# Layer 2 feed-forward of a four-layer transformer kernel, rewritten as one pipeline over sixteen units

## The reference

```python
x = x + _L2_ffn_ref(_layernorm(x, axis=-1), L2_ffn_w1, L2_ffn_conv_w, L2_ffn_conv_b, L2_ffn_w2)

def act_quant(x):                       # per token: 8 bit levels
    scale = 127.0 / jnp.clip(jnp.max(jnp.abs(x), axis=-1, keepdims=True), 1e-05)
    return jnp.clip(jnp.round(x * scale), -128, 127) / scale
def weight_quant(w):                    # -1, 0, 1 times one level
    scale = 1.0 / jnp.clip(jnp.mean(jnp.abs(w)), 1e-05)
    return jnp.clip(jnp.round(w * scale), -1, 1) / scale
# bit_linear(x, w) = act_quant(x) @ weight_quant(w).T
h = bit_linear(x, w1)                   # 128 features -> 512
h = depthwise_conv1d(h.transpose(0, 2, 1), conv_w, conv_b)   # 3 taps along the tokens of a sequence
h = jax.nn.silu(h.transpose(0, 2, 1))
return bit_linear(h, w2)                # 512 -> 128
```

## Time and profile before

| | us |
|---|---|
| median of 3 runs | 3416.47 |
| the profiled execution | 3413.9 |
| its span on the core | 3412.1 |
| from the first turn of the layer norm (2868.53) to the end of the last addition to xT (3047.40) | 178.9 |
| one chunk of 448 tokens (2968.00 to 3008.20) | 40.2 |
| VectorE busy in that chunk | 25.2 |
| TensorE busy in that chunk, at a granted clock of 0.50 | 15.3 |

### The profile page before, as it was taken

The page is one execution under the profiler, slowest core; times in us unless marked ns, Lnnn a source line. Parts: engine busy times, 40 slices in busy tenths (PEclk is TensorE's granted clock), DMA queues, the critical chain, the costliest instruction groups (busy, mean ns, idle before and its releaser), DMA issues. The chain is left out here.

```text
span 3412.1 us, 74955 instructions
## 1 busy us (share of the span) xinstructions
PE 3079.0 (90%) x30282; PEld 2137.9 (63%) x30282; DVE 2292.5 (67%) x4268; ACT 1742.8 (51%) x2862; POOL 1869.8 (55%) x1048
## 2 busy tenths in 40 slices
PE   7979989999999999999979998899999995349969
PEld 5654556777777777777757777455555553236644
DVE  4555557777777777777644443799999985654455
ACT  4534325666656666665644454366666663114545
POOL 0004556777777777777642220588888872014427
PEclk9979988999999999999989999799999996559989
DMA  7730016776666667767514665433333321304600
GB/s 142 145 114 22 1 37 125 139 147 130 134 137 142 130 134 139 142 131 140 111 51 154 235 236 218 98 99 98 96 96 92 92 69 36 55 0 93 135 1 12
DMA packets 607380, 367.70 MB, mean 108 GB/s; under 512 B 462933, under 2 KB 566626, under 8 KB 606786
## 3 DMA queue, kind: packets, MB, share of 16 engines
q1 hardware_dynamic: 607042, 362.96, 46.1%
HBM read 174.41 MB, written 75.24 MB: 73 GB/s over the span
## 5 line engine op out<-in xcount | busy, mean ns | idle before, releaser
L1742 POOL TENSOR_TENSOR L_plo<-L_p,L_phi 128x1500 bf16<-128x1500 f32 x224 | 659.1, 2943 | 295.0 <-DVE L_phi L1819 295.0
L1699 ACT COPY L_ptlo<-L_lt 128x1536 bf16<-128x1536 bf16 x224 | 322.1, 1438 | 407.6 <-PE L_lt L1623 407.6
L2121 ACT ACTIVATE L2b_p<-L2b_score 125x448 f32<-125x448 f32 x768 | 378.7, 541 | 273.2 <-PE L2b_score L2034 272.0
L1637 PE MATMUL L_acc<-L_chi,L_pthi 125*128 125x128 bf16 x2688 | 462.1, 219 | 0.0
L1639 PE MATMUL L_acc<-L_chi,L_ptlo 125*128 125x128 bf16 x2688 | 461.4, 219 | 0.0
L1638 PE MATMUL L_acc<-L_clo,L_pthi 125*128 125x128 bf16 x2688 | 461.2, 219 | 0.0
L1808 DVE TENSOR_SCALAR_CACHE_REDUCE L_p<-L_score,L_cols 128x1500 f32<-128x1500 f32 x224 | 395.4, 1765 | 84.8 <-PE L_score L1615 84.6
L1819 DVE CAST L_phi<-L_p 128x1500 bf16<-128x1500 f32 x224 | 298.1, 1331 | 164.6 <-ACT L_p L1693 163.7
L1693 ACT ACTIVATE L_p<-L_p,L_least 128x1500 f32<-128x1500 f32 x224 | 346.5, 1547 | 67.0 <-DVE L_p L1808 63.1
L2164 POOL TENSOR_TENSOR L2b_psum<-L2b_p 125x896 f32<-125x896 f32 x128 | 266.8, 2084 | 131.0 <-ACT L2b_p L2121 128.6
L2191 DVE TENSOR_REDUCE L2b_max<-L2b_m 112x1 f32<-112x1000 f32 x256 | 300.7, 1195 | 17.2 <-PE L2b_m L2015 9.5
(11 more groups left out here) (635 smaller groups left out, 6890.8 us busy)
## 6 DMA issues: line engine op xcount, KB each, us to landing
L2b_kst<-L_keys SPq DMA_DIRECT2D x96, 375.0 KB, 5.6
L_ct<-L_ct SPq DMA_DIRECT2D x32, 768.0 KB
L2a_ct<-L_ct SPq DMA_DIRECT2D x32, 768.0 KB, 15.1
L_ctx<-dram_ctx SPq DMA_DIRECT2D x32, 750.0 KB
L_keys<-L2a_kout SPq DMA_DIRECT2D x32, 750.0 KB, 8.0
L_values<-L2a_vout SPq DMA_DIRECT2D x32, 750.0 KB
L2b_vin<-L_values SPq DMA_DIRECT2D x32, 750.0 KB
L0x_ctx<-dram_ctx SPq DMA_DIRECT2D x32, 672.0 KB
```

What stands on the lines that cost most here:

```text
L1637: pe.matmul(acc, w_hi[0:KP, t, :], v_hi[0:KP, t, :], start=(t == 0), stop=False)
L1699: act.copy(pt_lo[g % 2][:, :, :], lt_ps[:, 0:KT * 128].rearrange("p (t q) -> p t q", t=KT)).then_inc(lo_read, 1)
L1742: pool.tensor_tensor(p_lo[g % 2][:, :, 0:KP], probs[g % RP][:, :].rearrange("q (t k) -> q t k", t=KT), p_hi[g % 2][:, :, 0:KP], ALU.subtra ...
L2121: act.activation(probs[t % RP][:, half * 2 * GW:(half + 1) * 2 * GW], score_ps[half][0:KP, 0:2 * GW], ACT.Exp).then_inc(exp_done, 1)
```

## The change

The three blocks become one, and the hardware loop is written out.

- **Front.** The layer norm's rows are not turned back as such. They are quantised where they lie (one token per partition, `quantise_rows`), in two halves of 8 and 6 tiles, and the rounded levels, in bf16, are turned (L2797 of the new file). The inverse scales of all tokens are spread at once: GpSimd makes 14 diagonals, TensorE multiplies them with ones, ScalarE reads four results into `inv_wide`. Weight quantisation and the clearing of the padded tiles lie among these steps; GpSimd also makes twelve 128x128 diagonals of the taps.
- **Taps.** The three taps of a unit (one block `j` of one chunk; 16 units) are three f32 products on TensorE with those diagonals, accumulated in PSUM. ScalarE applies Silu with the bias as it reads them.
- **Second quantisation.** Nothing is turned but one 128x448 tile per chunk: ScalarE writes the magnitudes of the four hidden blocks, VectorE takes their elementwise maximum, TensorE turns it, VectorE reduces it and makes two diagonals, TensorE spreads scale and inverse scale over the partitions, and VectorE scales and rounds the hidden values as they lie. The second product then leaves features on the partitions, and goes to `xT` without a turn.
- **Order.** One loop over m = 0 to 23 on every engine: units 0 to 15 in front, and behind them the quantisation of the chunk before and the product of the one before that.

```diff
--- before.py
+++ after.py
@@
-                    pe.wait_ge(silu_done, 4 * ch + 4)
-
-                    def to_tokens(k):
-                        wait(pe, quant2, 4 * ch + k - 1)
-                        for j in range(4):
-                            m = pe.transpose(zt_ps[k % 2][0:TOK, j * 128:(j + 1) * 128],
-                                             conv[j][:, k * TOK:(k + 1) * TOK], c["ident"][:, :])
-                        m.then_inc(zt_done, 1)
...
+                def up(m):
+                    ch, j = divmod(m, HID)
+                    pe.wait_ge(q1_ready, tiles_of(ch))
+                    wait(pe, pad_ready, m - 1)
+                    pe.matmul(up_ps[m % 2][:, 0:CH], wq[0][:, j * 128:(j + 1) * 128], q1T[:, cols(ch)], start=True,
+                              stop=True).then_inc(up_done, 1)
+
+                def conv(m):
+                    j = m % HID
+                    pe.wait_ge(pad_ready, m + 1)
+                    wait(pe, silu_done, m - 1)
+                    for t in range(3):
+                        ins = pe.matmul(conv_ps[m % 2][:, 0:CH].rearrange("p (b s) -> p b s", b=NB), taps[:, j, t, :],
+                                        pad[m % 4][:, :, t:t + S], start=(t == 0), stop=(t == 2))
+                    ins.then_inc(conv_done, 1)
...
+                def wide2(ch):
+                    pe.wait_ge(diag2_ready, ch + 1)
+                    wait(pe, scaled_done, HID * ch)
+                    wait(pe, inv2_read, ch)
+                    for ps, diag in ((scale_ps, diag_s), (inv_ps, diag_i)):
+                        ins = pe.matmul(ps[:, 0:CH], c["ones"][0:TOK, :], diag[:, :, :].rearrange("p k t -> p (k t)"),
+                                        start=True, stop=True)
+                    ins.then_inc(wide2_done, 1)
+
+                def product(ch):
+                    wait(pe, y_scaled, ch)
+                    for j in range(HID):
+                        pe.wait_ge(q2_ready, HID * ch + j + 1)
+                        ins = pe.matmul(y_ps[:, 0:CH], wq[1][:, j * 128:(j + 1) * 128], q2[j][:, :], start=(j == 0),
+                                        stop=(j == HID - 1))
+                    ins.then_inc(y_done, 1)
...
+                pe.wait_ge(wide1_read, NCH)
+                pe.wait_ge(w_ready, 2)
+                pe.wait_ge(taps_ready, HID)
+                pe.wait_ge(last_rows, 1)
+                up(0)
+                for m in range(UNITS + 2 * HID):
+                    ch, j = divmod(m, HID)
+                    if front(m + 1):
+                        up(m + 1)
+                    if front(m):
+                        conv(m)
+                    if j == 2 and 1 <= ch <= NCH:
+                        turn_largest(ch - 1)
+                    if j == 2 and ch >= 2:
+                        product(ch - 2)
+                    if j == 3 and 1 <= ch <= NCH:
+                        wide2(ch - 1)
...
+                def silu(m):
+                    ch, j = divmod(m, HID)
+                    act.wait_ge(conv_done, m + 1)
+                    wait(act, scaled_done, HID * (ch - 2) + j + 1)
+                    act.activation(hid[ch % 2][j][:, :], conv_ps[m % 2][:, 0:CH], ACT.Silu, bias=cb[:, j:j + 1]
+                                   ).then_inc(silu_done, 1)
+
+                def magnitude(m):
+                    ch, j = divmod(m, HID)
+                    act.wait_ge(silu_done, m + 1)
+                    wait(act, largest_step, 3 * (ch - 1) + max(j, 1) if ch else 0)
+                    act.activation(size[j][:, :], hid[ch % 2][j][:, :], ACT.Abs).then_inc(size_done, 1)
...
+                def quantise_rows(h):
+                    a, b = halves[h]
+                    st.link(dve.tensor_reduce(top1[:, a:b], rows[:, a:b, :], AX.X, ALU.max, apply_absolute_value=True))
+                    st.link(dve.tensor_scalar(top1[:, a:b], top1[:, a:b], 1e-5, None, ALU.max))
+                    dve.tensor_scalar(inv1[:, a:b], top1[:, a:b], 1.0 / 127.0, level[:, 0:1], ALU.mult, ALU.mult
+                                      ).then_inc(inv1_ready, 1)
+                    st.link(dve.reciprocal(scale1[:, a:b], top1[:, a:b]))
+                    st.link(dve.tensor_scalar(scale1[:, a:b], scale1[:, a:b], 127.0, None, ALU.mult))
+                    st.link(dve.tensor_tensor(rows[:, a:b, :], rows[:, a:b, :],
+                                              scale1[:, a:b].rearrange("p (t o) -> p t o", o=1
+                                                                       ).broadcast_to([128, b - a, D]), ALU.mult))
+                    dve.tensor_scalar(rounded[:, a:b, :], rows[:, a:b, :], MAGIC, MAGIC, ALU.add, ALU.subtract
+                                      ).then_inc(rounded_ready, 1)
...
+                def scales(ch):
+                    dve.wait_ge(largest_turned, ch + 1)
+                    st.link(dve.tensor_reduce(top2[:, :], largest_ps[0:TOK, :].rearrange("p (k d) -> p k d", k=NT), AX.X,
+                                              ALU.max, apply_absolute_value=True))
+                    st.link(dve.tensor_scalar(top2[:, :], top2[:, :], 1e-5, None, ALU.max))
+                    dve.tensor_scalar(inv2[:, :], top2[:, :], 1.0 / 127.0, level[0:TOK, 1:2], ALU.mult, ALU.mult)
+                    st.link(dve.reciprocal(scale2[:, :], top2[:, :]))
+                    st.link(dve.tensor_scalar(scale2[:, :], scale2[:, :], 127.0, None, ALU.mult))
+                    for diag, values in ((diag_s, scale2), (diag_i, inv2)):
+                        ins = dve.tensor_tensor(
+                            diag[:, :, :],
+                            c["ident"][0:TOK, 0:TOK].rearrange("p (o t) -> p o t", o=1).broadcast_to([TOK, NT, TOK]),
+                            values[:, :].rearrange("p (k o) -> p k o", o=1).broadcast_to([TOK, NT, TOK]), ALU.mult)
+                    ins.then_inc(diag2_ready, 1)
...
+                def scale_hidden(ch):
+                    dve.wait_ge(wide2_done, ch + 1)
+                    for j in range(HID):
+                        dve.tensor_tensor(scaled[j][:, :], hid[ch % 2][j][:, :], scale_ps[:, 0:CH], ALU.mult
+                                          ).then_inc(scaled_done, 1)
+
+                def round_hidden(ch):
+                    for j in range(HID):
+                        dve.wait_ge(scaled_done, HID * ch + j + 1)
+                        dve.tensor_scalar(scaled[j][:, :], scaled[j][:, :], MAGIC, MAGIC + 127.0, ALU.add, ALU.min
+                                          ).then_inc(grown_done, 1)
...
+                padded(0)
+                for m in range(UNITS + 2 * HID):
+                    ch, j = divmod(m, HID)
+                    if front(m + 1):
+                        padded(m + 1)
+                    if m >= 2 and front(m - 2):
+                        enlarge(m - 2)
+                    if j == 3 and 1 <= ch <= NCH:
+                        scales(ch - 1)
+                    if j == 3 and ch >= 2:
+                        output(ch - 2)
+                    if j == 0 and ch >= 2:
+                        scale_hidden(ch - 2)
+                    if j == 1 and ch >= 2:
+                        round_hidden(ch - 2)
```

More of the change, by code:

```diff
@@ L2748, in chunks @@
-        def chunks(eng, chunk):
-            chunk(0)
-            with eng.Fori(1, NCH) as ch:
-                chunk(ch)
+        made, pads_zero, taps_ready = sem("made"), sem("pads_zero"), sem("taps_ready")
+        w_summed, w_total_ready, level_ready, w_ready = sem("w_summed"), sem("w_total"), sem("level"), sem("w_ready")
+        turned, stats_done, parts_done, var_ready, rstd_ready, offset_ready = [
+            sem(n) for n in ("turned", "stats_done", "parts_done", "var_ready", "rstd_ready", "offset_ready")]
@@ L2910, in _, with statistics @@
-                for j in range(4):
-                    dve.memset(pad[j][:, :, :], 0.0)
-                dve.tensor_copy(ident_b[:, :], c["ident"][:, :]).then_inc(made, 1)
-                dve.wait_ge(made, 1)
-                chunks(dve, chunk)
+                st = Steps(dve, step)
+                def statistics(h):
+                    for g in (2 * h, 2 * h + 1):
+                        t0, n = groups[g]
+                        dve.wait_ge(turned, g + 1)
+                        for t in range(n):
+                            ins = dve.bn_stats(stats[:, t0 + t, :], x_ps[g][:, t * 128:(t + 1) * 128])
+                    ins.then_inc(stats_done, 1)
@@ new lines, in _ @@
+                ins.then_inc(w_summed, 1)
+                statistics(0)
+                variance(0)
+                statistics(1)
+                dve.wait_ge(w_total_ready, 1)
+                dve.tensor_scalar(level[:, :], inv_ps[:, 0:2], 1.0 / COUNT, 1e-5, ALU.mult, ALU.max
+                                  ).then_inc(level_ready, 1)
+                a, b = halves[0]
+                dve.wait_ge(rstd_ready, 1)
+                dve.scalar_tensor_tensor(offset[:, a:b], total[:, a:b], -0.5, rstd[:, a:b], ALU.mult, ALU.mult
```

(16 more changed lines are left out.)

381 lines of the change are left out of this document (195 added, 186 removed).

## The result

The changed kernel takes 3330.4 us (median of 4 runs, 3329.1 to 3331.5) against 3416.3 for the kernel before (4 runs, 3412.0 to 3417.1): a ratio of 0.9751, 95% interval 0.9739 to 0.9764. The profiled execution takes 3331.2, its span is 3329.2 and its mean clock 0.95. The forecast was 3335.6.

The account below looks back on a forecast made before the run. The stage was taken as a chain through engines taking turns, neither VectorE nor TensorE full. Front 23, units 52 and drain 23 make 98 against 178.9, 80.9 saved: 3333.0, plus 2.6 for the median, 3335.6 us; range 3324 to 3360.

Parts of the forecast that it names:

- Front: Stretch from the stage's first turn to the first padded tile: 23 us forecast, was 26.5.
- The term for quantising the rows: In the front, VectorE quantises eight tiles in 4.0 us, done at 14.1, and six in 3.2, done at 17.3.
- my choice between 23.8 and 22.3: Front's length with its last two spreading products at half clock (23.8) or full clock (22.3); 23 was taken.
- Units: Stretch from the first padded tile to the last tap product: 16 units of 2.44 us plus other work and waits, 52.
- The 1.5 for a lapse of the clock: In the units, 1.5 us added for a first unit at half clock or one lapse.
- the 0.7 for a late padding: In the units, 0.7 us more where a padded tile stands behind the scaling of hidden values.
- Drain: Stretch behind the last tap product, with VectorE nearly alone: 23 us forecast, 22.8 summed, 21.3 at full clock.
- Clock: TensorE's clock high in the units, low in parts of front and drain; transposes (turns) do not count as busy.
- Rivals 1 and 2: TensorE's clock falls at each wait for scales, 3350, chance 0.12; or stays low, 3374, chance 0.08.
- Rival 3: ScalarE reloads its tables between Silu and Abs in each unit: 20 us more, 3356, chance 0.03.
- Rival 4: Strided reading of padded tiles makes each tap product cost c; at c = 3.0 us the kernel takes 3437, chance 0.03.
- Rival 5: The gain is given back behind the stage, layer 3's attention being held by its loads: chance 0.02.

Follow-up runs that it names:

- the repeated execution: The changed kernel run once more with no edit: front 23.4 us, stage 93.4, median 3329.7 us.
- the last versions: Changed kernel with diagonals on ScalarE, scales spread diagonal by diagonal, reordered drain and earlier turn, 3320.8 us; with filling products on TensorE too, 3320.1 us.

## Why the prediction was right, step by step

- **Sum.** 98 forecast, 95.4 measured; 80.9 saved forecast, 83.5 measured by stage, 86.0 by medians. The errors have opposite signs, so the sum is closer than its parts: front +2.4, units -2.8, drain -2.2. The kernel came out 5.2 us under the forecast of 3335.6, and the stage is half of that. The other half is chance: I had put the median 2.6 above the profiled execution, and the new kernel's lies 0.8 under it, 3.4 less, of which small differences ahead of the stage and behind it take 0.8 back.
- **Front, 23 forecast, 25.4 measured.** The term for quantising the rows was mis-sized. Rows are complete at 9.8, where I had 10.1, but eight tiles took 5.6 instead of 4.0 and six took 4.9 instead of 3.2, because I set GpSimd's diagonals "beside it" and they hold VectorE: 1.7 and 1.6 of waiting inside the small steps. The halves end 1.3 and 2.9 later than in my sum, and so the rounding of the second half (20.2 us after the first turn) holds up TensorE's turns, where my sum had its first two spreading products do so. In the repeated execution the second pair at the high clock takes 2.0 of that back, and the front is 23.4; my choice between 23.8 and 22.3 for this pair was a choice between two things that both happen. Like for like the front was 1.6 late at the low clock (25.4 against 23.8) and 1.1 at the high one (23.4 against 22.3).
- **Units, 52 forecast, 49.2 measured.** 2.44 a unit is exact: strided reading of padded tiles costs what a flat one does (0.75 a product). The waits for scales were 1.6 each, 2 forecast. The 1.5 for a lapse of the clock and the 0.7 for a late padding were not needed.
- **Drain, 23 forecast, 20.8 measured.** Mis-sized were VectorE's rows in a row: from the start of a chunk's scaling to the start of its rounding 2.1 instead of 2.5, from there to the next step 2.4 instead of 3.0 (2.5 for the fourth chunk, 2960.71 to the end of the rounding at 2963.20), each twice, and the scales 2.5 instead of 2.9. VectorE was idle for 2.26 + 0.93 = 3.2 us, under the 5 that I had named.
- **Clock.** 1.00 through the units, 0.53 and 0.62 in front and drain, as expected. The turns of the rounded rows ran at 0.50 in the new kernel, and the clock rose behind f32 products only, as the rule on turns has it. Rivals 1 and 2 did not occur: the clock held through the waits of 1.6, while in the run with chunks in series the spread scales behind waits of 2.0 and 2.7 took 1.86, the low clock's time. Rival 3: one table load. Rival 4: c is 0.75 us, the flat price. Rival 5: layer 3's first product on its context on GpSimd begins at 2979.7, 14.3 after the stage, as it did before the change (3061.7, 14.3 after 3047.4), and nothing is given back.

Why the clock was high in one front and low in another of the same kernel stays open.

## What to carry to other kernels

When engines take turns, count what each would have to do if none waited, and take the largest as the bound: here TensorE's own work in the units, 45.2 us in the forecast, is what the last versions come down to (45.5). Then look at what runs beside what: an instruction of another engine is free only if the two do not hold each other up, and a tiny step that takes ten times its usual duration shows it. Small gains should be read from the stage in the trace, since a stage 7.5 us shorter showed as 0.6 in the median.

## What the runs showed of the hardware

- VectorE's step on 128 x 8 numbers stretched from 0.17 to 1.86 us beside a GpSimd product, and GpSimd's product from 1.89 to 2.80 beside VectorE's product of two tensors; with the same diagonals on ScalarE (14 instructions, 2.45 and 1.86 us) VectorE's step and product kept 0.17 and 1.22. VectorE's steps that read PSUM were not held by a GpSimd product (2.00 against 2.01). The recorded duration holds the waiting, so it doesn't appear as idle time.
- The same binary had TensorE at the low clock in one front and at the high clock in another, 2.0 us apart.
- Four instructions of 448 f32 columns in a row on VectorE took 2.21 (two tensors) and 1.29 (one tensor), 0.55 and 0.32 each, where a single one took 0.62 and 0.39: a sum of single durations overstates such a row by a tenth to a fifth.
